# Round one's soft threshold in a graph attention and Mamba block: ScalarE computes Relu(x - t), VectorE takes the smaller of x + t and it

## The reference

```
U = softmax(where(adj > 0, leaky_relu(f1 + f2.T), -inf), axis=1)      # 4096 x 4096
prop_u = U @ x
rowsum = sum(U * 0.5 * U, axis=1)
xi = x * rowsum[:, None]
feat = coe2 * (prop_u - xi) + (1 - coe2) * (x + prop_u - xi)
mod = abs(feat)
mod = where(mod > 1e-6, mod - 1e-6, 0.0)
feat = mod * sign(feat)                                               # soft threshold
pu = U @ feat                                                         # round two
...
x = x + gnn(layernorm(x));  x = x + mamba2(layernorm(x))
```

## Time and profile before

| | |
|---|---|
| runs of the kernel before | 782.66 us median of 3 (782.0 to 783.86) |
| profiled execution | 781.77 us, its span 780.0 us |
| granted TensorE clock, mean | 0.991 of full |
| round one, tiles 3 to 27 | from 98.4 to 309.9 us of the span |
| busy share of the span | PE 95%, DVE 93%, ACT 86%, POOL 81% |

### The profile page before, as it was taken

One profiled execution on the slowest core, in us unless ns is written; L12 is line 12 of the kernel. 1 busy time (PEld: TensorE's weight loads), 2 busy tenths in 40 slices (PEclk: granted clock), 3 DMA queues, 4 the chain that ended last, 5 costly groups with the idle time before them and its releaser, 6 DMA issues.

```text
span 780.0 us, 21076 instructions
## 1 busy us (share of the span) xinstructions
PE 737.7 (95%) x6049; PEld 707.6 (91%) x6049; DVE 726.2 (93%) x1898; ACT 670.5 (86%) x1428; POOL 628.5 (81%) x1215
## 2 busy tenths in 40 slices
PE   3679999999999999988899999999999999999987
PEld 1369999999999999987899999999999999999976
DVE  6999999999999999897999999999999999999986
ACT  5999898989899898976898989898989898989864
POOL 5584888888888888887888888888888888888863
PEclk9999999999999999999999999999999999999999
DMA  7689898989898986023121212121212121210000
GB/s 219 187 250 319 299 291 280 336 253 348 263 326 280 316 284 257 24 50 96 41 72 43 71 42 72 40 71 40 71 40 71 40 71 40 71 42 18 10 4 15
DMA packets 97962, 110.43 MB, mean 142 GB/s; under 512 B 6866, under 2 KB 89714, under 8 KB 97906
## 3 DMA queue, kind: packets, MB, share of 16 engines
q1 hardware_dynamic: 97906, 109.78, 43.5%
HBM read 90.87 MB, written 18.89 MB: 141 GB/s over the span
## 4 chain that ended last, share of the span: by engine, by line
PE 63%; DVE 22%; issue 6%; POOL 5%; ACT 3%; DVEq 1%; DMA 0%; ACTq 0%; POOLq 0%
PE accA L1708 21%; PE accC L1717 21%; DVE code L777 9%; DVE maskC L785 4%; PE ps L1818 3%; PE ps L1802 2%; PE ps L1835 2%; PE ps L1816 2%; PE ps L1820 2%; PE ps L1647 2%; PE ps L1854 2%; PE ps L1800 2%; PE ps L1827 1%; PE ps L1837 1%; PE ps L1843 1%
## 5 line engine op out<-in xcount | busy, mean ns | idle before, releaser
L1345 ACT ACTIVATE maskA<-code 128x1024 fp32r<-128x1024 int8 x256 | 269.2, 1054 | 20.5 <-DVE code L777 19.8
L1708 PE MATMUL accA<-Y,maskA 128*128 128x260 f32 (+1 forms) x1792 | 264.3, 290 | 1.6 <-ACT maskA L1345 1.2
L1717 PE MATMUL accC<-Y,maskC 128*128 128x260 f32 (+1 forms) x1792 | 253.4, 284 | 2.8 <-DVE maskC L785 2.7
L1708 PEld LDWEIGHTS accA<-Y,maskA 128*128 128x128 f32 x1792 | 231.5, 189 | 4.6 <-issue 2.3
L1717 PEld LDWEIGHTS accC<-Y,maskC 128*128 128x128 f32 x1792 | 229.2, 190 | 3.7 <-DVE maskC L785 3.6
L785 DVE TENSOR_SCALAR maskC<-code 128x1024 fp32r<-128x1024 int8 x256 | 206.6, 808 | 0.3
L777 DVE SCALAR_TENSOR_TENSOR code<-f_rows,neg_f,ps 128x512 int8<-128x512 int8 (+1 forms) x256 | 178.0, 738 | 0.3 <-DVE neg_f L741 0.2
L1282 ACT ACTIVATE edges<-adj_in 128x1024 int8<-128x1024 f32 x128 | 135.6, 1061 | 1.6 <-DMA adj_in<-in_adj_dram 1.6
L638 POOL TENSOR_TENSOR room_r<-room,room_r 128x256 fp32r<-128x256 f32 x128 | 97.7, 791 | 2.5
L1070 DVE SCALAR_TENSOR_TENSOR room<-room 128x128 f32<-128x128 f32 x270 | 86.3, 341 | 0.0
L1647 PE MATMUL ps<-ident,edges 128*128 128x128 bf16 x512 | 42.5, 223 | 12.0 <-ACT edges L1282 11.9
(11 more groups left out here) (275 smaller groups left out, 1622.2 us busy)
## 6 DMA issues: line engine op xcount, KB each, us to landing
adj_in<-in_adj_dram SPq DMA_DIRECT2D x128, 512.0 KB, 5.1
edge_codes<-code SPq DMA_DIRECT2D x32, 512.0 KB, 5.6
code<-edge_codes SPq DMA_DIRECT2D x32, 512.0 KB, 3.3
xn<-in_x_dram SPq DMA_DIRECT2D x4, 512.0 KB, 5.7
room<-in_x_dram SPq DMA_DIRECT2D x32, 64.0 KB, 1.8
room<-in_L_gnn_h_dram SPq DMA_DIRECT2D x32, 64.0 KB, 1.9
out_dram<-room SPq DMA_DIRECT2D x32, 64.0 KB, 1.6
room<-in_L_ffn_W_in_dram SPq DMA_DIRECT2D x1, 192.0 KB, 2.5
```

Source lines behind the costliest of these rows:

```text
L1345: s.activation(maskA[:, b % MASKS], src, ACT.Relu, bias=1.0 - LINK, scale=-1.0).then_inc(S["maskA_ready"], 1)
L1708: t_.matmul(accA[k][:, 0:2 * cols], maskA[:, b % MASKS, l * P:(l + 1) * P], y2_of(jt, 0) if cols == F else Y[:, jt, 0, :, 0:cols], start=j ...
L1717: m = t_.matmul(accC[k][:, 0:2 * cols], maskC[:, b % MASKS, l * P:(l + 1) * P], y2_of(jt, 1) if cols == F else Y[:, jt, 1, :, 0:cols], sta ...
```

## The change

Soft threshold is written as min(x + t, Relu(x - t)). A new ACT operation `above(T, k)` computes fwork[:, k] = Relu(scaled[:, k] - t), behind `mask1` at ch 2; DVE's feat1 becomes one scalar_tensor_tensor, (scaled + t) min fwork, and moves in the loop from ch 2 to ch 3. A semaphore `over_ready` goes from ACT to DVE. `fwork` had one half in use and now alternates. The feat1 of tile 29, behind the last supertile, stays as it was, and so do tiles 30 and 31.

```
 def feat1(T, k):
     wait(dve, "feat_done", T)
     dve.wait_ge(S["scaled_done"], T + 1)
-    inside = chain[0] > 0
-    link(v.tensor_scalar(fwork[:, 1], scaled[:, k], -THRESH, THRESH, ALU.max, ALU.min))
-    v.tensor_tensor(mine, scaled[:, k], fwork[:, 1], ALU.subtract).then_inc(S["feat_done"], 1)
-    if inside:
+    if isinstance(T, int) and T == NT - 3:
+        link(v.tensor_scalar(fwork[:, 1], scaled[:, k], -THRESH, THRESH, ALU.max, ALU.min))
+        v.tensor_tensor(mine, scaled[:, k], fwork[:, 1], ALU.subtract).then_inc(S["feat_done"], 1)
         dve.wait_ge(S["feat_done"], T + 1)
-    else:
-        end_chain()
+        return
+    dve.wait_ge(S["over_ready"], T + 1)
+    v.scalar_tensor_tensor(out=mine, in0=scaled[:, k], scalar=THRESH, in1=fwork[:, k], op0=ALU.add, op1=ALU.min).then_inc(S["feat_done"], 1)
...
 (DVE, supertile)
-        if ch == 2 and not (first and it < 2):
+        if ch == NB - 1 and not (first and it < 2):
             feat1(G * IT + (it - 2), it % 2)
...
+def above(T, k):
+    act.wait_ge(S["scaled_done"], T + 1)
+    wait(act, "feat_done", T - 1)
+    s.activation(fwork[:, k], scaled[:, k], ACT.Relu, bias=-THRESH, scale=1.0).then_inc(S["over_ready"], 1)
...
 (ACT, supertile, behind mask1)
+        if ch == 2 and not (first and it < 2):
+            above(G * IT + (it - 2), it % 2)
...
 (ACT, last supertile, behind mask1)
+    if ch == 2 and it < IT - 1:
+        above(G * IT + (it - 2), it % 2)
```

More of the change, by code:

```diff
@@ L231, in gnn_ffn_kernel @@
             f1col_done sums_done negf_ready fmax_done spread_done shift_done bias_ready ycol_hi ycol_done yA_prod yA_hi yA_done yC_prod yC_hi yC_done roww_done featsum_done colw_done f1_done f1_copied f1_out f1_laid ysum_done colmean_done coef_done
-            a1_ready adj_in0 adj_in1 adj_in2 adj_in3 signed tr_done coded maskA_ready maskC_ready mm_done acc_read summed
+            a1_ready adj_in0 adj_in1 adj_in2 adj_in3 signed tr_done coded maskA_ready maskC_ready mm_done acc_read summed over_ready
             spilled taken scaled_done feat_done pch vch codes_in0 codes_in1 codes_in2 codes_in3 y2_prod y2_prod_pool y2_hi y2_done y2_done_pool
```

## The result

The changed kernel takes 792.15 us (median of 4 runs, 791.3 to 793.18) against 783.26 us of the kernel before on the same chip (4 runs, 782.0 to 785.73). The ratio is 1.0116, with a 95% interval of 1.0099 to 1.0134: 8.9 us slower. The forecast was 790.5, range 784 to 795, that is 7.8 us over its base.

What follows compares the result with a forecast made beforehand. DVE was taken as the bound. Twelve pairs of tiles at 0.6 us gave 7.2, plus 1.0 in the last supertile, less 0.3 slack: 7.9 us over the profiled 781.77, about 789.7; plus 0.9 for the median, 790.5, range 784.0 to 795.0.

Steps and rivals of the forecast that it cites:

- The bound: In the loop before the change, DVE sets the pace at 70.4 us a pass; PE is some 0.8 us short of it.
- Relief: DVE's single threshold operation saves 0.32 us a tile; PE allows only 0.8 us a pass, at most 2.6 us in all.
- DVE's place: feat1 on DVE moves 1.92 us later in the loop, at no cost; up to 1.92 us a tile without POOL's cover.
- ACT, the work: The Relu on ACT takes 0.27 us, 1.1 us a supertile, hidden in ACT's wait of 2.7 us.
- ACT, the wait: At ch 2 the Relu waits for `scaled`, delaying the `edges` behind it; PE gets them 1.2 us late the first time.
- the ring: Circle of waits through POOL, ACT, PE and DVE in the loop: 18.2 us per two tiles, 0.6 over 17.6.
- Odd tiles: Odd tiles' rings decide, their POOL chain being longer by the sum of two tiles: 9.16 us against 8.82 or less.
- the signs that were named: Expected in the new trace: ACT waits 1 to 2 us per odd tile, PE about 0.6 per pair, pass about 72.8.
- The last supertile: The Relu's place in front of `y2_high` there costs 1.0 us, between bounds of 0 and 4.5.
- the 0.3 us for slack in the first pair: A deduction of 0.3 us from the summed loss of 8.2 us, for slack the first pair of tiles can use.
- the relief counts: Rival: with a POOL chain of 8.2 us from sum1, PE alone paces the loop, 780.0 us; chance 0.10.
- The rival that is slower still: Chain stays at 9.2 us, Relu costs 0.35, last supertile pays its full 4.5: 797 us; chance 0.12.

Runs made afterwards that it cites:

- late_relu: The changed kernel with the Relu one block later on ScalarE, at ch 3, in the loop and the last supertile: 781.78 us, 0.9994 of the kernel before.
- one_op: The changed kernel without the Relu and the wait for it, DVE's one operation leaving the threshold out: 778.24 us, 0.9953 of the kernel before.
- feat_late: The kernel before with its two threshold operations on DVE at ch 3 of the loop instead of ch 2: 781.97 us, 0.9996.
- relu_only: The kernel before plus an unused ScalarE Relu of the same size at ch 2, reading a constant tile without waiting for POOL: 782.02 us, 0.9996.
- old_last: The changed kernel in the loop, Relu at ch 2, with the last supertile as in the kernel before: 790.86 us, 1.0100 of the kernel before.
- no_featsum: The changed kernel without POOL's sum of two finished tiles in round one's odd tiles, its wait kept: 783.28 us, 1.0012 of the kernel before.
- late_relu_loop: The changed kernel with the loop's Relu at ch 3 and the last supertile as in the kernel before: 779.35 us, 0.9965 of the kernel before.
- wait_only: The kernel before plus only ScalarE's wait for POOL's `scaled` at the Relu's place, without a Relu: 793.37 us, 1.0141.

## Why the prediction was right

Point by point, by its own steps.

*The bound.* DVE before, PE 0.8 us a pass behind it: right. With DVE relieved and nothing put in the way, a pass is 69.55 us with PE busy throughout (late_relu).

*Relief.* "At most 2.6 us" was too small: one_op shows 3.8, the loop giving 2.4 of it (2.9 in late_relu). The new operation takes 0.29 us, as taken.

*DVE's place.* No cost, right (feat_late). It has a use which I did not see, 0.2 us off POOL's chain. The 0.34 us by which the new two-input operation could have lengthened the chain did not appear.

*ACT, the work.* Hidden, right (relu_only). The Relu takes 0.22 us start to start (127.09 to 127.31); I had taken 0.27.

*ACT, the wait.* The mechanism was right, and three kernels carry it: the wait alone gives the loss, the work alone gives none, and the loss moves with what is queued behind the wait (19.2, 18.3 and PE's 17.4 us for two tiles with the Relu ahead of the mask, behind it, one block later). The chain from sum1 to `scaled` was taken as 9.0 and is 8.98 and 8.87 in turns. Its terms: the start after `scaled` 0.03 for 0.11, the Relu 0.22 for 0.27, `edges` to the turn 1.17 for 1.11, turn to codes 4.71 for 4.45, codes to sum1 3.24 as taken. They give 18.35 against 18.2; over the loop it is 18.28.

The term that was too small is the one from PE's second turn to DVE's codes, and 0.18 of its 0.26 us is a slip of counting in the prediction. The four matmuls of one turn take 0.40 us (127.44), and the second turn of a pair starts 0.22 behind the first. From the start of a second turn to the end of the next pair's first turn is thus 4.35 - 0.22 + 0.40 = 4.53. The prediction put 4.35 there, which is the distance from one first turn to the next. In the new trace that end is 132.64 + 0.40 = 133.04, 4.56 after 128.48, and DVE starts 0.15 us behind it, at 133.19, where I had put 0.1. So the ring lost 7.8 us in the loop, where 7.2 were forecast.

*Odd tiles.* The waits of the Relu are in the odd ones, 12 of the 13 in the loop, 1.5 to 2.1 us from tile 5 on. The even tiles' chain is 7.7 to 7.9 us, and ACT reaches their Relu 0.8 to 0.9 us after `scaled`. Of the signs that were named, ACT's waits, PE's 0.64 us at the second turn and DVE's waits for turns came as written; the pass was put at 72.8 us and is 73.66.

*The last supertile.* 1.0 us was taken between bounds of 0 and 4.5. The traces have 2.9 for that stretch, of which old_last gives the Relu 1.7 (0.7 to 1.3 by the medians). The term was too small, and the 0.3 us for slack in the first pair was not there: that pair takes 18.35 us like the next.

*Where the sum was lucky.* The parts are less close than the total. The trace has 7.8 for the 7.2 and 2.9 for the 1.0 less 0.3; the medians, 8.9 us apart in these runs, stand nearer to the forecast of 7.9 than the traces' 10.1. And the loop's mean of 18.28 us for two tiles contains two pairs of 18.85, which no term foresaw, and a last pair of 17.50, which nearly make up for each other.

*The rivals.* That the relief counts did not come, but it is what the kernel gives with the Relu one block later. I had sought the turning point in a POOL chain of 8.2 us from sum1. no_featsum brings the odd tiles below it, to 7.9, and that takes the loss away but gives no gain (1.0012, loop 17.6 us for two tiles and not 17.4), by its timeline because the even tiles, at 8.0 to 8.4, then decide: the rival needed both chains to be short. The rival that is slower still was off: the chain did not stay at 9.2, and the last supertile did not pay its full 4.5.

The Trainium skill (Perfetto Trace Analysis, "Optimizing Scalar/DVE Operations") says that with a saturated DVE, offloading some work to Scalar "may make sense". It names no gain; the 780 us were my reading. The runs agree with the "may": moving the work gave 0.35% in late_relu_loop and a loss of 1.2% in the changed kernel, one block earlier in ScalarE's queue and in the last supertile too, on which the section says nothing.

The sign and the mechanism are shown by runs. That the wait alone costs 2.1 us more in the loop than wait and Relu together (0.17 for each of 12 pairs) adds up from the two timelines: 0.22 for the longer chain, 0.08 for small differences, less the 0.13 that the Relu costs in the ring. Not settled are the last 0.5 us that one_op gains and 1.2 us of the last supertile.

## What to carry to other kernels

Before an operation goes from a saturated engine to one with slack, look up in the trace when its input comes and when the other engine reaches the place: an in-order queue hands the wait to everything behind it. Here the slack (2.7 us per supertile) covered the work easily, and a wait of 1.5 us in every second tile cost 1.2% because the operation behind it fed PE. Then move the place: one block later took 1.2%, some 10 us, off, and where the receiving engine has no slack at all the old form was better (the last supertile, in which ScalarE was busy before for 30.1 of the 30.1 us from 309.9 to 340). It pays to add up the ring of waits across engines, since here its sum told the loss to about 1 us while every engine's busy share fell or stood. Where odd and even tiles have chains of different length, both rings must be added up.

## What the runs showed of the hardware

Where ScalarE waits for POOL's `scaled`, the Relu starts 0.03 us after its end (127.06 to 127.09) and an `edges` operation 0.11 after it (wait_only, 126.18 to 126.29); DVE needed 0.11 before. A Relu of 128x128 in float32 with constants for scale and bias takes 0.31 us, and the next operation starts 0.22 us after it. DVE starts 0.15 us after the end of the turn that it waits for in the ring above (133.04 to 133.19), and 0.04 in most other places; the ends of matmuls are modelled in the profile. In the pair of tiles at the end of the first and the second pass of the loop the ring is longer, 18.85 us for 18.1 to 18.35 in the other pairs but the last. There PE starts its next products 0.74 us after the second turn, with 0.34 us of idle time in which the profile shows nothing that it waits for; it took 0.23 us in the ring above (128.48 to 128.71):

```profile
164.94 0.40 PE L1657 MATMUL ps<-ident,edges 128*128 128x128 bf16 x4 [0.64 <-ACT edges L1282]
165.68 1.23 PE L1718 MATMUL accA<-Y,maskA 128*128 128x260 f32 x8 [0.34 <-issue]
```
